# Storing projection parts by row tile in a doubled DRAM buffer, and loading each operand stack with one DMA of 112 rows

## What is computed

```python
def _L0_attn_ref(x, w_qkv, w_out):          # 16 heads of 8
    q, k, v = ...                           # x @ w_qkv.T, split
    scores = jnp.einsum('bhtd,bhsd->bhts', q, k) * scale
    allowed = (j <= i) & (j >= i - WINDOW)  # WINDOW = 128
    attn = jax.nn.softmax(jnp.where(allowed[None, None], scores, -jnp.inf), axis=-1)
    ...
def _block(x, ...):
    h = _layer_norm(x, ln1_g, ln1_b)
    q, k, v = jnp.split(h @ w_qkv, 3, axis=-1)
    scores = jnp.einsum('bqhd,bkhd->bhqk', q, k) * hd ** (-0.5)
    ...                                     # causal mask, softmax, @ v, @ w_o, residual
    ...                                     # layernorm, gate, top 2 of 8 experts, gelu MLP of each, weighted sum
x = _layernorm(x + _L0_attn_ref(x, ...))
x = _layernorm(x + _L0_ffn_ref(x, ...))
```

## Time and profile before

| | |
|---|---|
| median of 3 runs | 786.75 us (780.8 to 787.21) |
| the profiled execution | 787.42 us |
| its span | 785.7 us |
| PE busy | 635.7 us (81%) |
| DVE busy | 577.1 us (73%) |
| ACT busy | 460.8 us (59%) |
| POOL busy | 424.0 us (54%) |
| DMA | 82.22 MB, mean 105 GB/s |

### The profile page before, as it was taken

The page is one execution under the profiler, slowest core; times in us unless marked ns, Lnnn a source line. Parts: engine busy times, 40 slices in busy tenths (PEclk is TensorE's granted clock), DMA queues, the critical chain, the costliest instruction groups (busy, mean ns, idle before and its releaser), DMA issues.

```text
span 785.7 us, 20471 instructions
## 1 busy us (share of the span) xinstructions
PE 635.7 (81%) x7679; PEld 390.0 (50%) x7679; DVE 577.1 (73%) x1308; ACT 460.8 (59%) x757; POOL 424.0 (54%) x643
## 2 busy tenths in 40 slices
PE   3578988989988788888879898988787997899850
PEld 1333544544444443444434343444337997899750
DVE  2555677777878989898889898988534775565676
ACT  2045665666766576767676767667663563555424
POOL 5026566567665444245546464656845555444663
PEclk8579999999999999999999999999979998999985
DMA  6744734744652625343535353510111223222505
GB/s 193 185 118 92 185 117 81 189 132 88 152 147 40 168 98 121 107 89 114 107 101 121 98 124 95 127 51 12 61 45 48 55 72 91 58 63 63 203 12 161
DMA packets 57549, 82.22 MB, mean 105 GB/s; under 512 B 7672, under 2 KB 48096, under 8 KB 54380
## 3 DMA queue, kind: packets, MB, share of 16 engines
q1 hardware_dynamic: 53132, 72.45, 35.9%
q0 software_dynamic: 4320, 8.47, 3.5%
HBM read 43.55 MB, written 37.17 MB: 103 GB/s over the span
## 4 chain that ended last, share of the span: by engine, by line
PE 43%; DVE 21%; DMA 9%; issue 9%; ACT 7%; POOL 4%; SPq 3%; another core or an unknown queue 1%; DVEq 0%; ACTq 0%; POOLq 0%
PE side_ps L1457 8%; PE pair_ps L1606 8%; PE pair_ps L1618 8%; DMA arena<-parts_dram 6%; PE pair_ps L1478 4%; PE pair_ps L1377 4%; DVE row_max L916 4%; ACT probs L745 4%; DVE row_max L918 3%; SPq L471 2%; DVE rest L939 2%; DMA arena<-shift_t 2%; PE side_ps L1517 2%; DVE row_max L921 2%; ACT parts L778 2%
## 5 line engine op out<-in xcount | busy, mean ns | idle before, releaser
L745 ACT ACTIVATE probs<-pair_ps 128x1024 f32<-128x1024 f32 x272 | 275.6, 1021 | 130.2 <-PE pair_ps L1377 123.0
L1457 PE MATMUL side_ps<-probs,v_aug 128*32 128x256 f32 (+3 forms) x2048 | 161.9, 411 | 7.8 <-POOL probs L650 3.0
L871 ACT ACTIVATE arena<-pair_ps,arena 128x128 f32<-128x128 f32 x284 | 80.9, 370 | 86.4 <-PE pair_ps L1606 55.5
L1377 PE MATMUL pair_ps<-arena 50*128 50x256 bf16 (+3 forms) x1024 | 107.7, 286 | 26.9 <-DMA arena<-shift_t 7.8
L637 POOL TENSOR_SCALAR_AFFINE_SELECT probs<-probs 128x512 f32<-128x512 f32 x96 | 61.4, 640 | 120.0 <-ACT probs L745 119.0
L703 POOL DMA_INDIRECT outputs_dram<-arena x71 | 70.6, 994 | 76.7 <-DVE arena L1262 55.3
L907 DVE TENSOR_REDUCE row_max<-pair_ps 128x4 f32<-128x768 f32 x96 | 89.0, 951 | 26.7 <-PE pair_ps L1411 26.1
L1606 PE MATMUL pair_ps<-arena 128*128 128x128 f32 x568 | 80.5, 287 | 21.7 <-DVE arena L1251 10.5
L1377 PEld LDWEIGHTS pair_ps<-arena 50*128 50x128 bf16 x1024 | 32.5, 95 | 108.5 <-issue 45.5
L1606 PEld LDWEIGHTS pair_ps<-arena 128*128 128x128 f32 x568 | 73.2, 201 | 24.6 <-issue 22.1
L916 DVE TENSOR_REDUCE row_max<-pair_ps 128x2 f32<-128x1024 f32 x64 | 76.5, 1219 | 7.4 <-PE pair_ps L1437 5.9
(11 more groups left out here) (177 smaller groups left out, 1049.9 us busy)
## 6 DMA issues: line engine op xcount, KB each, us to landing
arena<-parts_dram SPq DMA_DIRECT2D x96, 192.0 KB
parts_dram<-parts SPq DMA_DIRECT2D x32, 384.0 KB
parts_dram<-parts SPq DMA_DIRECT2D x32, 256.0 KB
pack<-in_pack SPq DMA_DIRECT2D x8, 578.0 KB
arena<-rows_dram SPq DMA_DIRECT2D x71, 65.0 KB
parts_dram<-parts SPq DMA_DIRECT2D x32, 128.0 KB
arena<-parts_dram SPq DMA_DIRECT2D x32, 128.0 KB
x_t<-in_x_t SPq DMA_DIRECT2D x8, 256.0 KB, 9.3
```

The source lines that it names most:

```text
L745: nc.scalar.activation(probs[:, n % PROBS, :], pair_ps[RING_AT["score", n][0]][:, :, :].rearrange("p b t -> p (b t)"), ACT.Exp, scale=SCAL ...
L871: last = nc.scalar.activation(hidden[n % H_DEPTH][:, f * BLK:(f + 1) * BLK], hidden_ps[n % 2][:, f * BLK:(f + 1) * BLK], ACT.Gelu_apprx_ta ...
L1377: last = nc.tensor.matmul(pair[:, r, col:col + width], k_st[u % STACKS][own, gs, j * P:(j + 1) * P], q_st[u % STACKS][own, gs, q0:q0 + wid ...
L1457: last = nc.tensor.matmul(o_ps[c * VHEAD:(c + 1) * VHEAD, q0:q0 + width], v_aug[u % 2][:, j, first:first + VHEAD], probs[:, slot, r * T + ...
```

## The change

The projection's columns are ordered row tile first (the weights are permuted on the host), so that partitions 0 to 63 of `parts` belong to row tile 0 and 64 to 127 to row tile 1. `parts_dram` becomes (2 buffers, 2 sides, 2 row tiles, 8 slots, 64, 512). Each side of a buffer is then 128 rows of 8 KB: 48 rows of row tile 0, 16 rows of ones (slots 6 and 7, written once at the start), 48 rows of row tile 1. One load of the first 112 of them fills a stack. The stores are split by row tile.

```diff
-SLOTS = 6
+SLOTS = HALF // HD
-STACK_LOADS = 5 * TILES_R * 16
+STACK_ROWS = HALF + STACK_K
+STACK_STORES = 2 * PARTS * TILES_R * 16
+STACK_LOADS = 2 * 16
+ONES_LOADS = (4 + STACKS) * 16
-        scratch = nc.dram_tensor("parts_dram", (2, SLOTS, P, T), BF16, kind="Internal").ap()
+        scratch = nc.dram_tensor("parts_dram", (2, 2, TILES_R, SLOTS, HALF, T), BF16, kind="Internal").ap()
+        def stack_rows(buffer, side):
+            return scratch[buffer, side].rearrange("r s (d g) t -> (r s d) (g t)", g=GS)
             sp.wait_ge(ones_made, 1)
+            for buffer in range(2):
+                for side in range(2):
+                    between = stack_rows(buffer, side)[STACK_K:HALF, :].rearrange("p (g t) -> p g t", t=T)
+                    sp.dma_start(between, ones_b[:, :].unsqueeze(1).to_broadcast(between.shape)).then_inc(ones_in, 16)
             for stack in k_st:
-                for r in range(TILES_R):
-                    sp.dma_start(stack[HALF * r + STACK_K:HALF * r + SCORE_K, :, :], ones_b[:, :]).then_inc(ones_in, 16)
+                sp.dma_start(stack[HALF + STACK_K:HALF + SCORE_K, :, :], ones_b[:, :]).then_inc(ones_in, 16)
@@ load_stacks(u), store(part, ready)
-                        place = scratch[side, slots[part]].rearrange("s p t -> p s t")
-                        sp.dma_start(place, parts[:, part, side, :].unsqueeze(1).to_broadcast(place.shape)
-                                     ).then_inc(stored_low if part else stored_high, 16)
+                        for r in range(TILES_R):
+                            place = scratch[u % 2, side, r, slots[part]].rearrange("s p t -> p s t")
+                            sp.dma_start(place, parts[HALF * r:HALF * (r + 1), part, side, :].unsqueeze(1).to_broadcast(place.shape)
+                                         ).then_inc(stored, 16)
@@ load_stacks(u)
-                if u:
-                    sp.wait_ge(stack_in[(u - 1) % STACKS], ((u - 1) // STACKS + 1) * STACK_LOADS)
+                if u >= 2:
+                    sp.wait_ge(stack_in[(u - 2) % STACKS], ((u - 2) // STACKS + 1) * STACK_LOADS)
...
-                sp.wait_ge(stored_high, (u + 1) * 32)
-                for side in range(2):
-                    load(side, *HIGH_ROWS[side])
-                sp.wait_ge(stored_low, (u + 1) * 64)
-                for side in range(2):
-                    for rows_of_part in LOW_ROWS[side]:
-                        load(side, *rows_of_part)
+                sp.wait_ge(stored, (u + 1) * STACK_STORES)
+                if u == 0:
+                    sp.wait_ge(ones_in, ONES_LOADS)
+                for side, stack in enumerate((q_st[u % STACKS], k_st[u % STACKS])):
+                    sp.dma_start(stack[0:STACK_ROWS, :, :].rearrange("p g t -> p (g t)"), stack_rows(u % 2, side)[0:STACK_ROWS, :]
+                                 ).then_inc(stack_in[u % STACKS], 16)
```

More of the change, by code:

```diff
@@ L68 @@
 PARTS = 3
-SLOTS = 6
+SLOTS = HALF // HD
 Q_SLOTS = (slice(0, 3), slice(4, 6), slice(3, 4))
 K_SLOTS = (slice(2, 5), slice(1, 6, 4), slice(0, 1))
-HIGH_ROWS = ((0, 24), (16, 40))
-LOW_ROWS = (((24, 48),), ((0, 16), (40, 48)))
 VPAD = 2 * HD
@@ L379, in build @@
         middle_ready, low_ready = sem("middle_ready"), sem("low_ready")
-        stored_high, stored_low = sem("stored_high"), sem("stored_low")
+        stored = sem("stored")
         stack_in = [sem(f"stack_in{i}") for i in range(STACKS)]
@@ L615, in plan_constants @@
             def plan_constants():
-                pool.wait_ge(stored_high, UNITS * 32)
-                pool.wait_ge(stored_low, UNITS * 64)
+                pool.wait_ge(stored, UNITS * STACK_STORES)
                 nc.gpsimd.memset(not_after, 1.0).then_inc(plan_consts, 1)
@@ L775, in high_part @@
                 if u:
-                    act.wait_ge(stored_high, u * 32)
-                    act.wait_ge(stored_low, u * 64)
+                    act.wait_ge(stored, u * STACK_STORES)
                 nc.scalar.activation(parts[:, 0, :, :], pair_ps[RING_AT["project", u][0]][:, :, :], ACT.Copy).then_inc(high_ready, 1)
@@ L1370, in scores @@
                     if u == 0:
-                        pe.wait_ge(ones_in, 2 * STACKS * 16)
+                        pe.wait_ge(ones_in, ONES_LOADS)
                 wait_ring("score", n)
@@ L1660 @@
     x = np.asarray(inputs["L0_attn_x"])
-    columns = [head(gs, r) * HD + d for d in range(HD) for r in range(TILES_R) for gs in range(GS)]
+    columns = [head(gs, r) * HD + d for r in range(TILES_R) for d in range(HD) for gs in range(GS)]
     weights = []
```

## The result

| kernel | median | runs | profiled execution | span | granted clock |
|---|---|---|---|---|---|
| before | 786.39 us | 780.8 to 787.21 | 787.42 us | 785.7 us | 0.936 |
| after | 803.49 us | 799.44 to 806.69 | 799.44 us | 797.7 us | 0.931 |

The ratio of after to before is 1.0216, with a 95% interval of 1.0181 to 1.025. The change makes the kernel 17 us slower by the medians; the profiled execution is after's fastest, and 12.0 us longer than the one of before. The forecast was 784 us with a range of 778 to 795. The median of before is of four executions; the 786.75 us ahead of the prediction is that of three of them.

The account below looks back on a forecast made before the run. PE's waits for the stacks were taken as the bound, at most 7.6 us outside the start; -0.2 + 0.2 + 1.7 + 0.2 + 0.5 + 0.4 = 2.8 us won, beside the median 783.9, gave 784 us, range 778 to 795.

Parts of the forecast that it names:

- h: In each unit, the end of the high part, from which the prediction measures every landing; 8.83 us in unit 0.
- h + 8.3: When all twelve stores of a unit have landed, with SP's issue setting the pace; bounds h + 7.5 and h + 9.2.
- 8.6 us for the loads: A unit's two stack loads: 0.4 us first issue, 2.0 latency, 6.2 data at 298 GB/s.
- h + 16.9: When a unit's stacks land, stores plus loads; bounds h + 15.3 and h + 20.9.
- My slow bound, h + 9.2: Latest landing of a unit's stores: 1.57 MB at 205 GB/s, with half a microsecond to land.
- Ones: Four start stores of ones, 0.5 MB, in SP's idle before unit 0's high part: free, or unit 0 up to 1 us later.
- the slow bound: Latest landing of a unit's stacks, h + 20.9: stores at 9.2, then 0.4 issue, 2.0 latency, 9.3 us of data.
- slower: narrow stores and later loads: Rival, 17%: stores at 205 GB/s, loads no faster per byte, stacks land at h + 20.9, 26 us lost, 813 us.
- threshold h + 18.2: Stack landing from which unit 4 begins to wait and units 3 to 7 pay in every iteration.
- half-way case: Slower rival at half its delay: stacks land at h + 19.2, 11 us lost, 798 us.
- The rule on ports: Skill page on 64-partition stores: 196 GB/s against 328 for 128; stores would end at h + 9.5, 1.2 us later.
- PE's needs: Stack landing PE needs: h + 14.9 in unit 2, h + 18.2 in unit 4, h + 17.9 in unit 7.

Follow-up runs that it names:

- the tail: Kernel before with groups of stores and loads, one shape per group, run on SP behind the last output; its total time says nothing.
- 64 + 64: Kernel before with each store cut into two of 64 partitions, same bytes: 846.86 us, ratio 1.0748.
- 96 + 32: Kernel before with each store cut into one of 96 and one of 32 partitions: 810.49 us, ratio 1.0279.
- two experiments on the old order: Kernel before with stores cut into 64 and 64 partitions, 846.86 us; kernel before with five small loads ahead of each unit's loads, 820.34 and 814.19 us.

## Why the prediction was wrong

**Two terms were too small, and both by a shape that the trace of before had not shown.** The forecast had h + 8.3 for the stores, 8.6 us for the loads and h + 16.9 for the landing. In unit 2 it is h + 10.35, 10.15 and h + 20.5: 2.05 us from the stores, 1.55 from the loads.

- *Stores, the term that failed first: "SP takes 0.42 us for one".* It is 0.61 (L472). I took an issue's price from another shape and weighed the shape only in the data. The last issue ends at h + 7.66 in unit 0, where the sum had h + 6.0. My slow bound, h + 9.2, came from data at 205 GB/s; SP alone put it at h + 9.7 to 10.8. That 64 partitions are a dear shape is shown by the tail, for one slot a store. That it costs time is the reading of three runs: 64 + 64 against 96 + 32, five small loads ahead of wide stores' loads, and two stores fewer in after.
- *Ones: "issued in the idle of SP ... costs nothing".* They take SP until 9.35, and the first store goes out at 9.40 where the high part ended at 8.95. Unit 0 is 0.45 us later by it, within the "up to 1 us" that I had put beside it.
- *Loads: "I take 341 x 112 / 128 = 298 GB/s, 6.2 us".* The tail has 261 GB/s for 112 rows and 424 for 128. The rate does not scale by the share of partitions. In unit 0 the whole leg was nonetheless right, 8.4 us for 8.6; in the later units it is 10.1. The sum let the loads run alone, and in unit 2 they don't: at 258 GB/s the 0.52 MB of the token loads are 2.0 us, an estimate from the window above, enough for the 1.55 us missing. No run takes the token loads away. Loads of 128 rows win 13 us, two stores fewer 11.
- *Landing.* h + 20.9 was the slow bound, and the units lie between h + 18.2 and h + 20.9: the slow end, on the path of the rival "slower: narrow stores and later loads". Its threshold h + 18.2 held, since unit 4 waits 2.96 us at h + 20.9, 2.7 by that rule. Its half-way case, h + 19.2 for 798 us, and its end, h + 20.9 for 813, enclose the 803.5 measured. I gave it 17%, on the ground that both terms had to be at their slow ends. They had not: the middle between the bounds, h + 15.3 and h + 20.9, is h + 18.1, at the threshold already, and for two shapes that no row shows I had no better value than the middle.

**The rule on ports.** With nothing else at work, the low half alone flows at 198 GB/s, the halves in turn at 267, the full width at 340. The Trainium skill (SBUF — State Buffer, "Door 1: The DMA port swizzle") gives 196 GB/s for the half and 328 for the whole, and both agree. The Trainium skill (SBUF — State Buffer, "Can I just issue two DMAs to hit both halves?") also says that two DMAs at once, one for each half, bring only 6% more than one. Here they bring 35% more, half of the gap. By the 196 GB/s of the Trainium skill the stores would end at h + 9.5, an estimate, and they ended at h + 9.7 in unit 0. But the chain gives SP's issue as the reason, with the data keeping up: the last store lands 2.04 us after its issue, where a wide one took 2.23.

**What was right.** PE's own waits are the place where the transfers count. Behind unit 10 the distances stay. Unit 1's wait goes, with the double buffer neutral. SP sets the pace of the stores. PE's needs (h + 14.9 in unit 2, h + 18.2 in unit 4) hold: after waits 5.66 in unit 2, and 20.5 - 14.9 = 5.6. One wait that I had not named came with the stores: ACT's high part of unit 1 stands 7.47 us for unit 0's stores to leave its buffer and runs 3.6 us later than before, but unit 1's stack is still in time.

**The price of being late** was about right for the change itself: 12.4 us more of waits in units 2 to 8 against 14.0 us in that stretch. It was far off for two experiments on the old order, 60 and 31 us lost. A part is TensorE's clock. The granted clock over the span is 0.936 before, 0.931 after and 0.890 with 64 + 64, which is 101, 110 and 186 us at the 1.2 GHz level in place of 2.4 (twice the missing share, times the span). With the small loads it is 0.916 and 0.918 in the two executions that count, 137 and 133 us. In three iterations of 64 + 64 the low clock shows as 12.8 us more of busy PE. Over the whole kernel an idle PE and a low clock come together in the rows, and the runs don't part the two. That stays open, as do the share of the late scatter of rows and why 64 partitions are dear to issue.

## What to carry to other kernels

When a change reshapes a DMA, price its issue and its rate for the new shape, and if no row has that shape, take the middle of the bounds and not the neighbour that is nearest in width. A load of all 128 partitions with rows that nobody wants can beat one of 112, and in the changed kernel one store with an odd stride beat two (in the kernel before it made no difference that could be told). And where loads are queued behind stores, count the slack of each unit first: with slack of 0 to 3 us, two microseconds on the issuing engine cost a per cent and more.

## What the runs showed of the hardware

- An issue on SP for exactly 64 partitions (or rows) took 0.60 us, against 0.36 to 0.44 for 16, 24, 32, 48, 96, 112 and 128 in groups of loads, of one-slot stores and of stores of 16 and 32 partitions. Of three-slot stores, 96, 112 and 128 partitions took 0.49 to 0.60 in the median, 64 took 0.62 to 0.63.
- Loads of 8 KB rows: 112 rows flow at 261 GB/s and 128 rows at 424, so that the larger load lands 2.3 us sooner.
- Small issues on SP ahead of the loads, 2.3 us in unit 0 and 3.0 in unit 2, in each of 16 units, cost 31 us.
- At a granted clock of 0.85 the same 399 matrix products kept PE busy for 39.3 us, and for 33.8 at 1.00.
